# Spectral stage of a two-layer kernel: another order of TensorE's pieces in a column, and the sum of the two accumulators on VectorE instead of GpSimd

## What is computed

```python
z   = (x - mu) / sqrt(var + 1e-5) * ln_gamma + ln_beta            # over channels
Xf  = rfft2(z)                                                    # 128 x 65 frequencies
U   = irfft2(Xf[:, :, None] * conj(Phi))                          # 16 filters, l = 0..15
S   = einsum('bdlxy,lhd->bhxy', U, Theta)
H   = gelu(einsum('bdxy,hd->bhxy', S, W1) + b1)
out = x + einsum('bhxy,dh->bdxy', H, W2) + b2
```

## Time and profile before

| what | value |
|---|---|
| three runs | 9360.18, 9369.12 and 9369.2 us, median 9369.12 us |
| the profiled execution | 9364.08 us, span 9362.3 us, mean granted TensorE clock 0.991 |
| PE busy (matmul) | 8641.8 us, 92% |
| VectorE busy | 8300.9 us, 89% |
| ScalarE busy | 7697.3 us, 82% |
| GpSimd busy | 8064.1 us, 86% |
| `sum_d` on VectorE (L1332) | 2470 operations, 743 ns each |
| `sum_p` on GpSimd (L1379) | 650 operations, 2390 ns each |
| `scaled` on ScalarE (L1290) | 1560 operations, 689 ns each |

### The profile page before, as it was taken

The page is one execution under the profiler, slowest core; times in us unless marked ns, Lnnn a source line. Parts: engine busy times, 40 slices in busy tenths (PEclk is TensorE's granted clock), DMA queues, the critical chain, the costliest instruction groups (busy, mean ns, idle before and its releaser), DMA issues. The chain is left out here.

```text
span 9362.3 us, 162156 instructions
## 1 busy us (share of the span) xinstructions
PE 8641.8 (92%) x54525; PEld 6730.2 (72%) x54525; DVE 8300.9 (89%) x8144; ACT 7697.3 (82%) x13926; POOL 8064.1 (86%) x3865
## 2 busy tenths in 40 slices
PE   7999999999999999999999999999799999999899
PEld 4666666666666666666666666666688888888788
DVE  5999999999999999999999999999788888888766
ACT  6999999999999999999999999999555555555577
POOL 5999999999999999999999999999688888888500
PEclk8999999999999999999999999999899999999999
DMA  3333333333333333333333333333201001000265
GB/s 92 109 121 114 111 119 111 118 112 121 114 111 118 112 118 112 121 114 111 118 112 118 112 121 114 111 118 110 76 32 37 32 32 36 33 32 32 80 188 181
DMA packets 648481, 931.99 MB, mean 100 GB/s; under 512 B 79960, under 2 KB 277600, under 8 KB 643552
## 3 DMA queue, kind: packets, MB, share of 16 engines
q1 hardware_dynamic: 647904, 924.64, 31.4%
HBM read 778.38 MB, written 146.04 MB: 99 GB/s over the span
## 5 line engine op out<-in xcount | busy, mean ns | idle before, releaser
L1035 POOL TENSOR_TENSOR prod<-state,c_all 128x1024 f32<-128x1024 f32 x1280 | 3027.8, 2370 | 73.0 <-DVE state L909 72.9
L1024 POOL TENSOR_TENSOR drive_d<-du,b_all 128x1024 f32<-128x1024 f32 x1024 | 2424.2, 2367 | 9.4 <-issue 7.5
L909 DVE TENSOR_TENSOR_SCAN state<-decay_d,drive_d 128x1024 f32<-128x1024 f32 x1024 | 2336.6, 2282 | 77.1 <-ACT decay_d L724 77.1
L909 DVE TENSOR_TENSOR_SCAN state<-decay_r,drive_r 128x1024 f32<-128x1024 f32 x1024 | 2323.4, 2269 | 28.2 <-PE drive_r L581 17.5
L594 PEld LDWEIGHTS y_acc<-ident,prod 128*128 128x128 f32 x16384 | 1864.8, 142 | 632.1 <-issue 524.6
L594 PE MATMUL y_acc<-ident,prod 128*128 128x128 f32 x16384 | 2157.8, 276 | 43.1 <-POOL prod L1035 39.4
L1332 DVE SCALAR_TENSOR_TENSOR sum_d<-bank_d,filt,sum_d 128x512 f32<-128x512 f32 x2470 | 1666.6, 743 | 251.7 <-PE bank_d L1240 251.4
L737 ACT ACTIVATE ub<-ut,bt 128x256 f32<-128x256 f32 x4096 | 1739.1, 500 | 12.4 <-PE drive_r L581 12.0
L1379 POOL TENSOR_TENSOR sum_p<-sum_p,scaled 128x1024 f32<-128x1024 f32 x650 | 1553.4, 2390 | 210.9 <-ACT scaled L1290 173.6
L1290 ACT ACTIVATE scaled<-bank_p,filt 128x512 f32<-128x512 f32 x1560 | 945.4, 689 | 889.4 <-PE bank_p L1240 886.4
L724 ACT ACTIVATE decay_d<-delta,neg_a 128x504 f32<-128x504 f32 x2048 | 1312.1, 674 | 79.7 <-DVE state L909 78.7
(11 more groups left out here) (155 smaller groups left out, 14620.6 us busy)
## 6 DMA issues: line engine op xcount, KB each, us to landing
c_all<-bc_rows SPq DMA_DIRECT2D x1280, 256.0 KB, 3.3
b_all<-bc_rows SPq DMA_DIRECT2D x1024, 256.0 KB, 3.9
ys<-row_spectra SPq DMA_DIRECT2D x130, 256.0 KB, 2.8
column_sums<-tt SPq DMA_DIRECT2D x130, 256.0 KB, 2.1
x_in<-in_x_dram SPq DMA_DIRECT2D x64, 512.0 KB, 5.0
x_res<-in_x_dram SPq DMA_DIRECT2D x64, 512.0 KB, 5.0
x_rows<-x SPq DMA_DIRECT2D x64, 512.0 KB, 4.6
row_spectra<-z SPq DMA_DIRECT2D x64, 512.0 KB, 3.7
```

Of the source, the lines that this page charges most:

```text
L909: dve.tensor_tensor_scan(state[n % NT][:].rearrange("p h t -> p (h t)"), decay[:].rearrange("p h w t -> p (h w t)"), drive[:].rearrange("p ...
L1024: pool.tensor_tensor(drive_d[place_of(DSTEPS, n, ND)][:], du[:, :, q * HT:(q + 1) * HT], b_all[slot][:].unsqueeze(1).to_broadcast([P, 2, HT]),
L1035: pool.tensor_tensor(prod[n % NP][:], state[n % NT][:], c_all[slot][:].unsqueeze(1).to_broadcast([P, 2, HT]), ALU.mult).then_inc(s["prod_g ...
```

## The change

TensorE's pieces stand in another order, one unit changes from u = 11 to u = 12 (so that the p units are 1, 4, 6, 9, 12 and 14), VectorE's `split_x` move to behind d2 and d7, and `mix` moves from the front of GpSimd's column to VectorE, behind its third unit d2 and ahead of `split_x` of pair 0. A seventeenth step at the end of a column holds the second `inverse`. The number of matmuls, of scalings and of additions is the same.

```diff
-BY_POOL = (1, 4, 6, 9, 11, 14)
+BY_POOL = (1, 4, 6, 9, 12, 14)
 BY_DVE = [u for u in range(UNITS) if u not in BY_POOL]
-COLUMNS = {5: 0, 11: 1}
-BACK = {7: 0, 13: 1}
-SPLIT_AFTER = (4, 8)
+COLUMNS = {3: 0, 11: 1}
+BACK = {8: 0, UNITS: 1}
+MIX_AFTER, SPLIT_AFTER = 2, (2, 7)
@@ TensorE (ScalarE's loop likewise)
-                for u in range(UNITS):
+                for u in range(UNITS + 1):
                     if col and u in COLUMNS:
                         columns(k + 1, half + p, 1 - p, COLUMNS[u])
                     if back and u in BACK:
                         inverse(k - 1, BACK[u])
-                    if products:
+                    if products and u < UNITS:
                         unit(k, p, u)
@@ VectorE
+            def mix(k, p):
+                need(dve, s["summed_p"], (k + 1) * STEPS)
+                need(dve, s["summed_d"], (k + 1) * ND * OPS)
+                need(dve, s["inv_done"], k * 2)
+                dve.tensor_tensor(mixed[:], sum_d[p][:].rearrange("p c b h -> p c (b h)"), sum_p[p][:],
+                                  ALU.add).then_inc(s["mixed_done"], 1)
                 for n in range(ND):
                     if products:
                         sum_unit(k, p, n)
+                    if back and n == MIX_AFTER:
+                        mix(k - 1, 1 - p)
                     if columns and n in SPLIT_AFTER:
                         split_x(k + 1, 1 - p, SPLIT_AFTER.index(n))
@@ GpSimd: the same mix is taken out
-                if back:
-                    mix(k - 1, 1 - p)
```

## The result

The changed kernel takes 9387.34 us (median of 12 runs, 9382.99 to 9392.74) against 9363.62 us before (12 runs, 9358.17 to 9369.2): a ratio of 1.0025 with a 95% interval of 1.0017 to 1.0034, or 23.7 us more. Its profiled execution took 9386.8 us with a span of 9385.0, 22.7 more than that of before. The forecast was 27 more.

A forecast was written before the change was run, and what follows sets the result against it. A cycle of TensorE and VectorE waiting in turn was taken to set the 32.17 us column. The new column, 32.62, adds 63 x 0.45 = 28.4 us, less 1.2 at the stage's end: +27 on 9364.08, 9391 us, range 9374 to 9412.

The forecast's parts named there:

- The two waits: TensorE before p2 and p5: waits until ScalarE has read `bank_p`, 1.33 us more twice a column, plus 0.11 each.
- s: Time from the end of a p unit on TensorE to ScalarE's first scaling: taken as 0.28 us, 0.20 in the last column.
- the walk: Piece-by-piece timing of one new column on TensorE, with VectorE's beside it: 32.62 us against 32.17 before.
- The rest of the walk: TensorE's other pieces: needed VectorE results arrive in time, d5 tightest at 0.9 us slack; old waits of 1.1 and 0.8 go.
- The 11 us that the range kept for the loop's edge: Range allowance for TensorE crossing the loop's edge every second column without a stall: a third of the bound, 31 x 0.35.
- The sum on VectorE: The mix, one 128x1024 addition moved from GpSimd: 1.23 us, some 1.14 to the next start, covered by VectorE's idle time.
- The rule on the shared port: VectorE's two-SBUF-input mix contends with GpSimd's SBUF reads; whichever starts first keeps the port for its whole length.
- The rival built on it: GpSimd's p1 addition goes first, mix ends 2.4 us later, d5 1.8 late: 9490 to 9505 us; chance 0.06.
- The faster rival: ScalarE's reads of `bank_p` do not hold TensorE: 29.74 us a column, 153 us less, 9210; chance 0.06.
- The near end: Both `bank_p` stalls occur with ScalarE starting 0.20 us behind TensorE: +17 us, 9381; chance 0.16.

## Why the prediction was right

**Sign and size.** +23.7 us measured, +27 forecast, 9387 in a range of 9374 to 9412. On the profiled executions, which the sum went by, it is 9386.8 against 9391.

**The two waits.** Right, with the row that priced them: the wait of the last column of before is that of every column after, 1.08 and 1.16 us in the record. The term that was mis-sized is s, the start of ScalarE behind TensorE. I took 0.28 for both, and it was 0.21 for p1 and 0.28 for p4. That is 0.07 a column, 32.55 in place of 32.62, and 4 us of the sum; the beat was 32.54. The reason I gave, that s is larger in a column with `columns` pieces, is wrong, and the trace of before could have told: I compared p1 of the last column (0.20) with p5 of a steady one (0.28), and p1 of that steady column begins at 0.20 too (7162.62 to 7162.82). So it goes by the unit, not by the column. With 0.20 for p1 and 0.28 for p4 the walk gives the measured 32.54. Why p1 is served sooner, no run here settles.

**The rest of the walk.** Right: the second `x_low` and the old wait on `sum_d` went, TensorE starts a column behind i1 with a unit of 1.82, and d5 and d6 found their banks free. The beat from 7158.91 to 7191.45 is made up of the pieces at their old prices and the two waits, with nothing left over, and the mean beat of 60 columns is the same 32.54, so neither the short entries of weight loads on `sum_d` nor the edge of the loop cost anything. The 11 us that the range kept for the loop's edge were not needed. VectorE was idle less than forecast, 2.9 us a column and not 3.5, and GpSimd as forecast, 5.4 against 5.5; TensorE's column loses nothing to either.

**The sum on VectorE.** 1.22 us in the record, 1.23 worked out from 512 and 2048 elements, 1.13 to the next start (7169.70 to 7170.83 on VectorE). It costs nothing in this order, as the run with the sum on GpSimd shows.

**The rule on the shared port.** The prediction left it open, since no row of before had such a pair. The Trainium skill (SBUF — State Buffer, Who interferes with whom) has the second of the two stand still for the first one's whole length; the trace agrees, from both sides: 2.66 us for a sum that came second, 3.35 for an addition that did. The rival built on it needed GpSimd to start p1 before VectorE reached the sum. The prediction gave that 0.20 us of margin, and the trace shows 0.14. So the contention is real and only the order kept it harmless: one step later (the sum behind d3) there was a loss, though by way of i0 and not of d5, and its 160 us are 130 of waiting and 30 of a lower clock. That the rival stayed away with 0.14 us to spare is a close call and not proof that a chance of 0.06 was right.

**The faster rival**, a bank that can be refilled while ScalarE reads it, is out by the longer reading, which came back twice a column in full. **The near end**, +17, would have needed 0.20 both times; with 0.20 once and 0.28 once the walk gives +22, halfway between it and the forecast.

## What to carry to other kernels

Where units of work share one buffer, write the order so that the time from one to the next on the producing engine is at least the start and the length of the reader, here 2.7 us or two units; one step of one unit was worth 52 us in 9,390. A wait that steady columns never show may stand in the first or last column, where pieces are missing: look there for its price. Before a two-input addition is moved to the other of VectorE and GpSimd, look which instruction of the one will run when the other arrives, and who waits for the later one.

## What was not expected of the hardware

**Behind some of the longer waits TensorE's clock fell for a while.** In the changed kernel, with waits of 1.1 to 1.2 us, the granted clock is 1.00 from 6800 to 8650, and so it is in the kernel before and in every other kernel here whose waits are no longer than that. With waits of 1.8 to 1.9 us in front of the inverse (the sum behind d3) it was not, in some columns. The timeline of TensorE behind one such wait:

```profile
7210.49 1.12 PE L1249 MATMUL way<-mixed,ix 128*128 128x512 f32 x2 [1.91 <-DVE mixed L1355]
7211.45 1.56 PE L1250 MATMUL way<-mixed,ix 128*128 128x512 f32 x2
7212.02 1.20 PE L1240 MATMUL bank_d<-th_high,x_high 128*128 128x256 f32 x1
7213.02 0.42 PE L1240 MATMUL bank_d<-th_low,x_high 128*128 128x256 f32 x1
7213.23 0.42 PE L1240 MATMUL bank_d<-th_high,x_low 128*128 128x256 f32 x1
```

Matmuls start every 0.21 us there and not every 0.12, and the busy times by stretch give the clock (last three columns: granted clock, DMA share, GB/s):

```profile
7210.00:7211.50 1.50, 1.01 (x3) 0.54 (x4) 1.50 (x3) 0.00 (x0) 1.50 (x1) 1.00 0.00 1
7211.50:7215.30 3.80, 3.80 (x15) 2.98 (x14) 1.50 (x3) 0.60 (x1) 3.45 (x2) 0.55 0.03 6
7215.30:7220.00 4.70, 4.70 (x35) 4.49 (x34) 4.28 (x7) 2.42 (x4) 1.57 (x1) 1.00 0.00 0
```

0.55 is near the lower of the two levels, 1.2 GHz, for 3.8 us. Of ten such waits between 7032 and 7357, three were followed by it. The distances between the starts of `mixed` give the price over the whole stage: 18 of 62 columns take 36.2 to 36.4 us, the others 34.6 in the mean, which is 1.65 us each time, 0.5 us a column, and the 30 us over the expectation. With ScalarE's reading in eight parts, where the waits on `bank_p` are 1.7 and 1.76 us, it came in some columns as well:

```profile
7236.00:7240.00 4.00, 3.16 (x27) 2.96 (x25) 3.58 (x7) 2.16 (x7) 2.83 (x2) 1.00 0.00 0
7240.00:7244.00 4.00, 3.08 (x15) 3.08 (x16) 2.56 (x4) 1.00 (x4) 3.92 (x2) 0.63 0.02 4
```

There it came in every fourth column for nearly the whole stage: 15 of 62 columns take 35.2 to 35.3 us and the others 33.75, and 1.5 us in every fourth is its 0.36 a column. So where each wait grew from 1.1 to 1.7 us, a column became 1.6 us longer and not 1.2. These are the only two kernels here with such waits and the only two in which the clock fell in steady columns; that the waits bring it about is concluded from that, and no run lengthened a wait step by step. What decides in which columns it happens stays open.
